# A 16-batch attention and quantised feed-forward kernel: later load slots, a piecewise-contiguous low-rank factor, and a new instruction order

## The chip, the cores and the metric

The kernel runs on one core of one Trainium2 chip. The metric is the device time in microseconds (us) of one execution. Before the change it is 500.97 us, the median of three runs (500.2 to 503.21).

The engines are TensorE (PE, its weight loads are PEld), VectorE (DVE), ScalarE (ACT), GpSimd (POOL) and SyncE (SP), which here only issues DMAs.

## The reference

For 16 batches of x (128 tokens x 512) with a context of 128 x 128:

```python
x = x + attention(layernorm(x), ctx, ctx, q_norm_w, k_norm_w, w_out)   # 16 heads of 32, 4 key heads, rotary, causal
w_up = ((w_up_q - 7.5) * repeat(w_up_scale, 64, axis=1)).T             # 512 x 2048, int32 in memory
y1 = h @ w_up + b_up + h @ w_up_lora_a @ w_up_lora_b                   # h = layernorm(x), rank 16
x2 = relu(y1)
y2 = x2 @ w_down + b_down + x2 @ w_down_lora_a @ w_down_lora_b         # w_down: 2048 x 512, 4 bit likewise
x = x + y2
```

Attention normalises queries and keys by their root mean square, applies the rotary rotation, a causal mask and softmax, and multiplies by w_out.

## The kernel before

**Tiling.** Every float32 product is made of three float16 products (high by high, low by high, high by low). The weights are dequantised once, on the chip, into 32 tiles of 128 x 512: tiles 0 to 15 are the up layer, 16 to 31 the down layer, four tiles to a group of 1 MB that one DMA brings (`load_group`, L346; the staging ring has three places). A weight tile costs: the dequantisation (DVE L1040, or POOL L450 and L453), the turn on PE (`weights`, L801: one low-rank product of 512 columns at L814, then four 128 x 128 float32 transposes at L762 into the same bank), the high part (ACT L615), and the low part, either by DVE (L1048) or by a product with minus the identity (`weights_rest`, L825, product at L830) and a copy on ACT (L620). The low-rank factor of the up layer, `b_up3`, is scaled and split in four pieces by `lora_b_high` (ACT, L604) and `lora_b_low` (DVE, L1023); in its 512 columns the token order is "p then i", and L811 reads it as `(p i) -> i p`, each fourth element.

**Batches.** Each of the 16 batches goes through: statistics, rotary parts, the query and key transposes by DMA (`qT` L396, `kT` L382), four score products S (L856), mask and maximum (DVE L1146), exponentials (ACT L658), probabilities (POOL L480, L489), their transposes by DMA (L406), PV (L872), the output projection PJ (L884, 12 products), the second normalisation and its transpose `xnT` (L389), four up products UP.0 to UP.3 (L902, 12 products of 512 columns each), the hidden layer (DVE L1077, ACT L723, DVE L1086), its transposes (L414), four down products DN.0 to DN.3 (L916, 12 products each), and the store.

**What sets the order.** All engines walk the same counter, `for s in range(SLOTS)`. Each step has a row of slots (`R_...`): three for batches 0 to 2, and one from which batch 3 and all later ones follow every 264 slots. Each weight step has its slot in `TURN_AT`, `DEQ_AT`, `HIGH_AT`, `LOW_AT`, `REST_AT`, `LOAD_AT` and so on. A slot is only a place in the order of an engine's queue; it is no time, and semaphores do the rest. An instruction that waits holds everything behind it on its engine, and on SP a waiting DMA holds the later ones. Below, "W12" is the turn of tile 12 on PE, "S2.1" the second score product of batch 2, and PV1, PJ1, UP1.0, DN0.3 are named the same way.

**The queue of SP.** Before slot 0 SP issues (L356 to L373) batch 0, the small operands, groups 0 and 1, batch 1, group 2, w_out (1 MB), batches 2 and 3, the broadcast bias row (1 MB) and the down bias. Then come the transposes kT0 and qT0; group 3 follows when W3 is done.

**The order of PE** that the tables before give, from PV0 to UP1.0 (sums of squares "v"): PV0, rest 7, rest 8, PJ0, W11, S1.3, W12, v2, W13, W14, W15, rest 12, rest 13, W16, W17, UP0.0, W18, S2.0, W19, S2.1, UP0.1, W20, W21, UP0.2, PV1, W22, S2.2, W23, S2.3, UP0.3, W24, PJ1, W25, DN0.0, W26, W27, DN0.1, W28, W29, S3.0, S3.1, v3, W30, W31, DN0.2, DN0.3, S3.2, UP1.0.

Of the kernel before, what the change touches and what calls it, by code (L numbers as in the profile page):

```python
# [1268 lines left out]
```

## Time and profile before

| | |
|---|---|
| median of three runs | 500.97 us (500.2 to 503.21) |
| the profiled execution, its own time | 503.2 us |
| its span, first to last instruction | 501.4 us |
| PE busy | 458.9 us (92%) |
| DVE, ACT, POOL busy | 343.9 (69%), 303.7 (61%), 292.7 (58%) |
| mean granted TensorE clock | 0.990 |
| PE in the chain that ended last | 85% of the span |

The span is what the rows below are counted in; the execution's own time is 1.8 us more, which lies around it. Row times are from the span's start.

### The profile page before, as it was taken

What the parts mean: (1) busy time and instruction counts of PE and PEld (TensorE: products, weight loads), DVE (VectorE), ACT (ScalarE), POOL (GpSimd) and SP (SyncE); (2) the same over time, 40 slices, a digit from 0 to 9 for tenths busy, and PEclk for the clock granted to TensorE, in tenths of its full rate; (3) what the DMA queues carried; (4) which work ended last, traced back from release to release, by engine and by line L of the source; (5) the groups of instructions that cost most, each with busy time, mean ns of one, the idle gap of its engine ahead of it and who ended that gap; (6) DMA issues with size and microseconds to landing.
All of it is one profiled execution on the core that took longest, in us unless ns stands there. A gap on an engine that the chain in (4) does not pass through costs nothing.

```text
span 501.4 us, 8264 instructions
## 1 busy us (share of the span) xinstructions
PE 458.9 (92%) x2413; PEld 221.6 (44%) x2413; DVE 343.9 (69%) x1082; ACT 303.7 (61%) x927; POOL 292.7 (58%) x304
## 2 busy tenths in 40 slices
PE   0157788999999999999999999999999999999997
PEld 0135434455444444444444444444444444444443
DVE  2759889898768687777777777676767676443341
ACT  1469987568767675757575757676666666521110
POOL 3435764577776758585768585767676756460101
PEclk9999997899999999999999999999999999999999
DMA  7884447936788776777887778778768678474523
GB/s 141 330 242 124 89 151 190 209 74 127 122 173 136 146 138 116 162 127 148 140 148 150 137 150 134 156 125 161 141 143 147 138 118 134 87 136 74 106 46 100
DMA packets 207853, 70.41 MB, mean 140 GB/s; under 512 B 197809, under 2 KB 200113, under 8 KB 207121
## 3 DMA queue, kind: packets, MB, share of 16 engines
q1 hardware_dynamic: 205472, 69.33, 68.4%
q10 hardware_dynamic: 2256, 0.40, 0.5%
q8 instruction: 19, 0.31, 0.3%
q14 instruction: 26, 0.20, 0.1%
q0 software_dynamic: 80, 0.16, 0.1%
HBM read 17.44 MB, written 4.19 MB: 43 GB/s over the span
## 4 chain that ended last, share of the span: by engine, by line
PE 85%; ACT 3%; DVE 2%; DMA 1%; issue 1%; SPq 0%; ACTq 0%
PE ff L916 33%; PE ff L902 33%; PE tb L884 8%; PE ff L762 3%; PE sb L856 3%; PE tb L872 3%; PE ff L814 2%; DMA qT<-q 1%; ACT pr L658 1%; ACT b_row L588 1%; DVE pr L1146 1%; ACT wo_hi L577 0%; PE tb L842 0%; ACT wu_hi L615 0%; DVE wu_lo L1048 0%
## 5 line engine op out<-in xcount | busy, mean ns | idle before, releaser
L902 PE MATMUL ff<-wu_hi,xnT 128*128 128x512 f16 x512 | 153.4, 381 | 0.0
L916 PE MATMUL ff<-wd_hi,x 128*128 128x512 f16 x512 | 152.3, 379 | 0.0
L658 ACT ACTIVATE pr<-pr,nmax 128x128 f32<-128x128 f32 x256 | 99.0, 388 | 33.6 <-DVE nmax L1146 33.3
L1146 DVE CUSTOM_DVE_ANT_0 pr<-sb,tabs,score_scale 128x128 f32<-128x128 f32 x256 | 74.1, 344 | 43.1 <-POOL big L489 22.8
L723 ACT ACTIVATE hid<-z 128x512 f16<-128x512 f32 x64 | 40.2, 628 | 99.0 <-DVE z L1077 99.0
L902 PE MATMUL ff<-wu_lo,xnT 128*128 128x512 f16 x256 | 97.4, 380 | 0.0
L916 PE MATMUL ff<-wd_lo,x 128*128 128x512 f16 x256 | 97.0, 379 | 0.0
L480 POOL TENSOR_TENSOR pr<-pr,rinv 128x512 f32<-128x512 f32 x64 | 72.8, 1152 | 22.1 <-DVE rinv L1056 22.0
L489 POOL TENSOR_TENSOR big<-pr,big 128x512 f16<-128x512 f32 x64 | 75.2, 1185 | 7.7 <-ACT big L689 7.7
L902 PEld LDWEIGHTS ff<-wu_hi,xnT 128*128 128x128 f16 x512 | 48.5, 98 | 59.2 <-issue 7.0
L1077 DVE SCALAR_TENSOR_TENSOR z<-ff,su,b_row 128x512 f32<-128x512 f32 x64 | 47.8, 747 | 37.3 <-PE ff L902 36.0
L916 PEld LDWEIGHTS ff<-wd_hi,x 128*128 128x128 f16 x512 | 49.3, 100 | 51.8
L519 POOL TENSOR_TENSOR inv<-arg,minus_half 128x1 f32<-128x1 f32 x16 | 14.2, 886 | 83.8 <-DVE arg L1132 83.8
L1086 DVE SCALAR_TENSOR_TENSOR hid<-z,hid 128x512 f16<-128x512 f32 x64 | 52.4, 818 | 14.3 <-ACT hid L723 13.2
L658 ACT ACTIVATION_READ_ACCUMULATOR pr<-pr,nmax 128x1 f32 x256 | 48.0, 187 | 0.0
L902 PEld LDWEIGHTS ff<-wu_lo,xnT 128*128 128x128 f16 x256 | 25.1, 98 | 30.6 <-issue 0.6
L916 PEld LDWEIGHTS ff<-wd_lo,x 128*128 128x128 f16 x256 | 25.0, 98 | 30.3
L529 POOL TENSOR_TENSOR y<-x,bd_bc 128x512 f32<-128x512 f32 x16 | 23.7, 1482 | 24.9 <-DMA out<-y 24.8
L689 ACT ACTIVATE big<-pr 128x512 f16<-128x512 f32 x64 | 37.8, 615 | 0.0
L762 PE MATMUL ff<-tabs,big 128*128 128x128 f32 x128 | 29.6, 370 | 2.0 <-DVE big L1040 1.8
L856 PE MATMUL sb<-kT,qT 96*128 96x128 f16 x256 | 24.9, 230 | 5.2 <-DMA qT<-q 5.2
L512 POOL TENSOR_TENSOR t_cos<-xc,cw 128x512 f32<-128x512 f32 x16 | 25.9, 1616 | 3.8 <-ACT xc L629 3.7
(147 smaller groups left out, 622.9 us busy)
## 6 DMA issues: line engine op xcount, KB each, us to landing
xt<-in_x SPq DMA_DIRECT2D x16, 256.0 KB, 3.1
big<-in_L_ffn_w_up_q SPq DMA_DIRECT2D x4, 1024.0 KB, 6.0
big<-in_L_ffn_w_down_q SPq DMA_DIRECT2D x4, 1024.0 KB, 5.6
...
wd_lo<-in_L_xattn_w_out SPq DMA_DIRECT2D x1, 1024.0 KB, 11.7
pT<-in_L_ffn_b_up SPq DMA_DIRECT2D x1, 1024.0 KB, 12.8
pT<-big SPq DMA_TRANSPOSE x64, 3.5
```

The lines of the kernel that those rows point to most:

```text
L480: pool.tensor_tensor(pr[:, m], pr[:, m], rinv[:, p, 4 * m:4 * m + 4].unsqueeze(2).broadcast_to([P, NG, P]), ALU.mult).then_inc(probs, 1)
L489: pool.tensor_tensor(p3[:, m, :, 1, :], pr[:, m], p3[:, m, :, 0, :], ALU.subtract).then_inc(p_low, 1)
L658: last = act.activation(pr[:, m, g, :], pr[:, m, g, :], ACT.Exp, bias=nmax[:, p, j:j + 1], scale=-1.0, accum_out=rsum[:, p, j:j + 1])
L723: act.activation(hid[:, (4 * n + g) % HID_RING, 0, :], z[:, g % 2], ACT.Relu).then_inc(x2_high, 1)
L762: return pe.matmul(dst, src, ident[0:src.shape[0], 0:src.shape[0]], is_transpose=True, **kw)
L856: last = pe.matmul(sbk[m % 2][:, P * g:P * g + P], qT[0:HD3, 4 * m + g, :], kT[0:HD3, g, :], start=True, stop=True)
L884: last = pe.matmul(tb[0][:], a[:, m, :], b[:, m, :], start=(i == 0 and m == 0), stop=(i == 2 and m == NN - 1))
L902: last = pe.matmul(bank[:], a[:, m, :], b[:, m, 512 * g:512 * g + 512], start=(m == 0 and i == 0), stop=(m == KC - 1 and i == 2))
L916: last = pe.matmul(ff[down_bank[n]][:], x2T[:, part, k + h % HG, :], b[:, h, :], start=(h == 0 and i == 0), stop=(h == HC - 1 and i == 2))
L1077: dve.scalar_tensor_tensor(z[:, g % 2], ff[up_bank[n, g]][:], su[:], b_row[:, 512 * g:512 * g + 512], ALU.mult, ALU.add).then_inc(ff_read, 1)
L1086: dve.scalar_tensor_tensor(h[:, 1, :], z[:, g % 2], 0.0, h[:, 0, :], ALU.max, ALU.subtract).then_inc(x2_low, 1)
L1146: last = dve.tensor_tensor_reduce(pr[:, m, g, :], sbk[m % 2][:, P * g:P * g + P], mask, score_scale[:], 3e38, ALU.add, ALU.min, nmax[:, p, ...
```

## The change

Three things change.

1. **Loads.** Group 2, w_out, batches 2 and 3, the bias row and the down bias are no longer issued before slot 0 but in slots of their own. SP's order becomes: batch 0, the small operands, groups 0 and 1, batch 1, then w_out, batch 2, qT0, group 2, kT0, the down bias, the bias row, qT1, kT1, groups 3 and 4, the four pT of batch 0, group 5, kT2, qT2, group 6, xnT0, batch 3, group 7, batch 4.
2. **The low-rank factor.** `b_up3` is written in the order in which it is used, so the product at L814 reads 512 neighbouring elements, and the reordering moves into the source operand of the eight small steps that fill it (L604 and L1023, up pieces).
3. **The order.** All slots are new. DVE dequantises 26 tiles instead of 25 (POOL six instead of seven) and makes 27 low parts instead of 28; the tiles whose low part goes through PE and ACT are 7, 9, 10, 12, 13 instead of 7, 8, 12, 13. No products are added to keep PE busy.

The order of PE from S1.1 to UP1.0 is now: S1.1, S1.2, rest 7, S1.3, W10, rest 9, W11, PV0, W12, W13, rest 10, PJ0, W14, rest 12, W15, v2, W16, W17, S2.0, rest 13, S2.1, W18, W19, S2.2, UP0.0, W20, UP0.1, W21, S2.3, W22, UP0.2, W23, PV1, W24, UP0.3, W25, W26, PJ1, W27, DN0.0, W28, W29, DN0.1, W30, W31, S3.0, v3, S3.1, DN0.2, DN0.3, S3.2, UP1.0.

The diff, cut to its core (the other tables change in the same way):

```diff
-R_SCORES = ((26, 270, 777, 1283), (104, 312, 811, 1320), (119, 390, 924, 1386), (188, 447, 954, 1463))
-R_PV = (412, 879, 1518, 1745)
-R_PROJ = (433, 1065, 1522, 1799)
-R_XNTURN = (705, 1434, 1720, 1991)
-R_UP = ((748, 1406, 1732, 1999), (815, 1471, 1740, 2003), (876, 1504, 1787, 2026), (990, 1519, 1814, 2066))
-R_DOWN = ((1103, 1539, 1886, 2113), (1183, 1546, 1903, 2153), (1363, 1574, 1910, 2191), (1384, 1725, 1922, 2199))
...
+R_SCORES = ((78, 338, 891, 1411), (140, 412, 909, 1440), (198, 451, 980, 1515), (227, 457, 1065, 1544))
+R_PV = (584, 1143, 1556, 1854)
+R_PROJ = (702, 1259, 1615, 1866)
+R_XNTURN = (878, 1405, 1740, 2015)
+R_UP = ((986, 1532, 1788, 2102), (1021, 1535, 1839, 2114), (1097, 1554, 1841, 2119), (1201, 1608, 1865, 2175))
+R_DOWN = ((1286, 1623, 1914, 2216), (1348, 1671, 1962, 2280), (1458, 1694, 2012, 2289), (1500, 1710, 2039, 2306))
...
-DVE_TILES = (0, 1, 2, 3, 4, 5, 6, 7, 8, 9, 11, 15, 16, 17, 18, 19, 20, 21, 22, 23, 24, 25, 27, 28, 29)
-LOW_BY_DVE = (0, 1, 2, 3, 4, 5, 6, 9, 10, 11, 14, 15, 16, 17, 18, 19, 20, 21, 22, 23, 24, 25, 26, 27, 28, 29, 30, 31)
-TURN_AT = (14, 37, 40, 111, 215, 310, 325, 339, 366, 407, 411, 443, 457, 551, 562, 602, 707, 719, 773, 780, 830, 863, 906, 935,
-           991, 1097, 1142, 1160, 1236, 1277, 1344, 1357)
-HIGH_AT = (58, 73, 271, 276, 306, 367, 422, 451, 499, 546, 618, 684, 726, 782, 797, 810, 834, 840, 890, 942, 965, 966, 1037,
-           1088, 1147, 1158, 1193, 1224, 1285, 1292, 1316, 1329)
-REST_AT = (0, 0, 0, 0, 0, 0, 0, 427, 432, 0, 0, 0, 679, 702, 0, 0, 0, 0, 0, 0, 0, 0, 0, 0, 0, 0, 0, 0, 0, 0, 0, 0)
-LOAD_AT = (20, 484, 595, 711, 855)
-LORA_TURN_AT = (2, 4, 15)
-LORA_BHIGH_AT = (8, 9, 10, 364, 517)
-LORA_BLOW_AT = (8, 15, 25, 472, 603)
-WO_TURN_AT = (162, 170, 236, 256)
-WO_HIGH_AT = (129, 146, 193, 256)
-BIAS_ROW_AT = (171, 253, 296, 316)
-WO_SQUARES_AT, WO_SUM_AT, WO_ARG_AT, WO_POW_AT = 11, 6, 17, 7
...
+DVE_TILES = (0, 1, 2, 3, 4, 5, 6, 7, 8, 10, 11, 12, 13, 14, 15, 17, 18, 19, 21, 23, 25, 26, 27, 28, 29, 31)
+LOW_BY_DVE = (0, 1, 2, 3, 4, 5, 6, 8, 11, 14, 15, 16, 17, 18, 19, 20, 21, 22, 23, 24, 25, 26, 27, 28, 29, 30, 31)
+TURN_AT = (67, 115, 121, 215, 253, 350, 352, 356, 388, 410, 463, 550, 586, 612, 778, 803, 873, 877, 910, 953, 992, 1058, 1070,
+           1115, 1150, 1207, 1242, 1277, 1313, 1318, 1383, 1409)
+HIGH_AT = (76, 187, 192, 203, 217, 356, 369, 380, 410, 442, 516, 587, 626, 697, 751, 772, 843, 859, 943, 1014, 1058, 1113, 1169,
+           1201, 1262, 1359, 1395, 1445, 1469, 1478, 1501, 1581)
+REST_AT = (0, 0, 0, 0, 0, 0, 0, 453, 0, 530, 663, 0, 796, 900, 0, 0, 0, 0, 0, 0, 0, 0, 0, 0, 0, 0, 0, 0, 0, 0, 0, 0)
+LOAD_AT = (61, 462, 490, 770, 861, 906)
+WO_LOAD_AT, ROW_LOAD_AT, DOWN_BIAS_LOAD_AT = 2, 262, 169
+BATCH_LOAD_AT = (3, 881)
+LORA_TURN_AT = (2, 6, 108)
+LORA_BHIGH_AT = (8, 9, 40, 41, 453)
+LORA_BLOW_AT = (15, 24, 73, 117, 513)
+WO_TURN_AT = (174, 175, 207, 289)
+WO_HIGH_AT = (104, 107, 188, 226)
+BIAS_ROW_AT = (167, 266, 290, 357)
+WO_SQUARES_AT, WO_SUM_AT, WO_ARG_AT, WO_POW_AT = 13, 3, 34, 132
...
@@ -291,7 +293,8 @@
             if by_dve:
                 eng.wait_ge(w_low_v, by_dve)
 
-        b_pieces = [(b_up3[:, 512 * i:512 * i + 512], b_up_in[:, 512 * i:512 * i + 512], 4) for i in range(4)] + [(b_dn3, b_dn_in, 5)]
+        b_pieces = [(b_up3[:, 512 * i:512 * i + 512].rearrange("k (i p) -> k i p", i=4),
+                     b_up_in[:, 512 * i:512 * i + 512].rearrange("k (p i) -> k i p", i=4), 4) for i in range(4)] + [(b_dn3, b_dn_in, 5)]
 
 
         tile_bank, up_bank, down_bank, tile_free, up_free, down_free = {}, {}, {}, {}, {}, {}
@@ -365,12 +368,6 @@
             load_group(0)
             load_group(1)
             load_batch(1)
-            load_group(2)
-            sp.dma_start(wo_raw, wo.rearrange("(j p) c -> p j c", p=P)).then_inc(wout_in, 16)
-            load_batch(2)
-            load_batch(3)
-            sp.dma_start(bias_raw, bu.rearrange("(a n) -> a n", a=1).broadcast_to([P, H])).then_inc(bias_row_in, 16)
-            sp.dma_start(bd_bc[:], bd.rearrange("(a n) -> a n", a=1).broadcast_to([P, C])).then_inc(down_bias_in, 16)
             sp.wait_ge(parts_empty, 2)
             for s in range(SLOTS):
                 n = at(s, R_KTURN)
@@ -412,9 +409,18 @@
                         if n > 0:
                             sp.wait_ge(down_done, n)
                         sp.dma_start_transpose(x2T[:, g], hid[:, (4 * n + g) % HID_RING].rearrange("p a h -> p (a h)")).then_inc(x2_turned[g], 16)
-                for g in range(W_RING, 8):
-                    if LOAD_AT[g - W_RING] == s:
+                for g in range(2, 8):
+                    if LOAD_AT[g - 2] == s:
                         load_group(g)
+                if s == WO_LOAD_AT:
+                    sp.dma_start(wo_raw, wo.rearrange("(j p) c -> p j c", p=P)).then_inc(wout_in, 16)
+                for n in (2, 3):
+                    if BATCH_LOAD_AT[n - 2] == s:
+                        load_batch(n)
+                if s == ROW_LOAD_AT:
+                    sp.dma_start(bias_raw, bu.rearrange("(a n) -> a n", a=1).broadcast_to([P, H])).then_inc(bias_row_in, 16)
+                if s == DOWN_BIAS_LOAD_AT:
+                    sp.dma_start(bd_bc[:], bd.rearrange("(a n) -> a n", a=1).broadcast_to([P, C])).then_inc(down_bias_in, 16)
                 n = at(s, R_STORE)
                 if n is not None:
                     store(n)
@@ -808,7 +814,7 @@
                     pe.wait_ge(b_high, t // 4 + 1)
                     pe.wait_ge(b_low, t // 4 + 1)
                 if t < UP_TILES:
-                    a, b = a_up3[:, P * j:P * j + P], b_up3[:, 512 * g:512 * g + 512].rearrange("k (p i) -> k i p", i=4)
+                    a, b = a_up3[:, P * j:P * j + P], b_up3[:, 512 * g:512 * g + 512]
                 else:
                     a, b = (a_dn3[:], a_dn3_late)[t // 24][:, P * (t % 8):P * (t % 8) + P], b_dn3
                 pe.matmul(bank[:], a, b, start=True, stop=False, skip_group_check=True)
```

## Rows read from the trace of the kernel before

**Rows 1.** Busy time by stretch: length, PE, PEld, DVE, ACT, POOL, clock, DMA

```profile
36.00:60.00 24.00, 17.54 (x75) 12.02 (x74) 21.42 (x73) 22.78 (x66) 14.23 (x15) 1.00 0.36 90
60.27:82.25 21.98, 20.57 (x88) 10.17 (x89) 18.32 (x38) 17.72 (x45) 12.14 (x14) 0.84 0.56 154
82.25:125.64 43.39, 41.64 (x223) 21.94 (x221) 38.12 (x115) 30.70 (x95) 28.75 (x32) 0.96 0.75 150
125.64:498.15 372.51, 372.28 (x1999) 172.87 (x1996) 246.59 (x790) 217.77 (x696) 222.03 (x216) 1.00 0.71 132
```

**Rows 2.** The chain that ended last, in order of time

```profile
79.46 7.38 DMA qT<-q
...
101.44 2.59 PE ff L902 x12
...
105.03 2.59 PE tb L884 x12
...
190.40 0.45 PE sb L856 x8
...
498.15 0.75 DVE y L1196
```

**Rows 3.** What PE waited for in the first 130 us

```profile
PE sb L856 <- DMA qT<-q: 5.2, 3, 2.3
PE sb L774 <- ACT big L571: 3.7, 1, 3.7
```

**Rows 4.** PE in order of time: start, length, step

```profile
63.33 0.61 PE L814 MATMUL ff<-wd_lo,wd_hi 48*128 48x512 f16 x1
63.87 1.12 PE L762 MATMUL ff<-tabs,big 128*128 128x128 f32 x4
...
66.31 1.03 PE L830 MATMUL ff<-wu_hi,minus 128*128 128x512 f16 x2
67.81 1.04 PE L884 MATMUL tb<-wo_hi,oT_hi 128*128 128x512 f16 x4 [0.46 <-DVE oT_lo L1167]
...
72.88 0.61 PE L814 MATMUL ff<-wd_lo,wd_hi 48*128 48x512 f16 x1 [0.95 <-ACT wu_lo L620]
73.41 0.66 PE L762 MATMUL ff<-tabs,big 128*128 128x128 f32 x4
...
87.35 0.38 PE L856 MATMUL sb<-kT,qT 96*128 96x128 f16 x4 [1.35 <-DMA qT<-q]
...
93.11 0.39 PE L814 MATMUL ff<-wd_hi,a_dn 48*128 48x512 f16 x1
...
94.11 0.39 PE L814 MATMUL ff<-wd_hi,a_dn 48*128 48x512 f16 x1
```

**Rows 5.** PE by stretch: length, busy, granted clock, DMA

```profile
75.00:76.00 1.00, 1.00 (x5) 0.50 0.93 363
```

**Rows 6.** The low-rank product of line L814, by form: ns min/median/max

```profile
L814 PE MATMUL ff<-wd_lo,wd_hi x16: 606/607/609, 30.4 to 77.3; 48*128 48x512 f16 x16
L814 PE MATMUL ff<-wd_hi,a_dn x8: 386/387/605, 79.7 to 100.2; 48*128 48x512 f16 x8
```

**Rows 7.** ACT from 20 to 100 us, by line and form

```profile
L588 ACT ACTIVATE b_row<-pT,kap 128x512 f32<-128x512 f32 x4 | 4.8, 1201 | 0.0
L604 ACT ACTIVATE wd_lo<-wd_hi,kap 48x512 f16<-48x512 f32 x4 | 2.6, 706 | 0.0
```

**Rows 8.** SP's queue in order of time

```profile
24.36 8.15 SPq L396 DMA_TRANSPOSE qT<-q  x1
...
78.98 0.37 SPq L350 DMA_DIRECT2D big<-in_L_ffn_w_down_q  x1
```

**Rows 9.** DMA issues by line: KB each, median us to landing

```profile
qT<-q SPq DMA_TRANSPOSE x16, 4.4
xnT<-xn_parts SPq DMA_TRANSPOSE x16, 3.1
wd_lo<-in_L_xattn_w_out SPq DMA_DIRECT2D x1, 1024.0 KB, 11.7
```

More of the change, by code:

```diff
@@ L68 @@
[L68 to L73 removed]
+R_STATS = (0, 6, 40, 928)
+R_SQUARES = (2, 6, 280, 1133)
@@ new lines @@
+R_MOMENTS = (0, 12, 220, 1073)
+R_KEYS = (0, 4, 202, 1453)
+R_POW = (2, 19, 463, 1494)
+R_CENTRE = (3, 44, 376, 1227)
+R_SINES = (2, 44, 308, 1194)
+R_COSINES = (3, 57, 625, 1592)
+R_ROPE = (3, 46, 437, 1215)
+R_KSPLIT = (4, 154, 441, 1334)
+R_KLOW = (4, 85, 421, 1235)
+R_KTURN = (85, 439, 799, 1300)
+R_QSPLIT = (5, 117, 574, 1376)
+R_QLOW = (5, 77, 557, 1262)
+R_QTURN = (54, 380, 806, 1253)
+R_SCORES = ((78, 338, 891, 1411), (140, 412, 909, 1440), (198, 451, 980, 1515), (227, 457, 1065, 1544))
@@ new lines @@
+R_MASK = ((35, 258, 702, 1446), (50, 319, 716, 1459), (121, 386, 996, 1471), (159, 560, 1122, 1537))
+R_EXP = ((98, 444, 1057, 1586), (169, 500, 1112, 1599), (262, 742, 1329, 1663), (340, 862, 1373, 1772))
+R_SUMS = ((49, 415, 1146, 1490), (86, 556, 1175, 1530), (173, 570, 1366, 1661), (233, 788, 1448, 1713))
+R_PROBS = ((182, 651, 1595, 1911), (193, 657, 1599, 1925), (411, 879, 1645, 2013), (484, 1099, 1839, 2080))
+R_PHIGH = ((207, 673, 1374, 1691), (229, 815, 1449, 1753), (375, 995, 1557, 1842), (390, 1080, 1592, 1861))
@@ new lines @@
+R_PLOW = ((327, 737, 1621, 1947), (379, 973, 1628, 1964), (564, 1300, 1790, 2038), (577, 1382, 1857, 2136))
+R_PTURN = ((509, 1062, 1273, 1748), (634, 1135, 1412, 1769), (694, 1143, 1435, 1774), (706, 1148, 1471, 1780))
+R_VSUM = (337, 398, 849, 1432)
+R_VARG = (172, 283, 945, 1507)
+R_VPOW = (456, 649, 1837, 2135)
+R_VSPLIT = (393, 1189, 1603, 1871)
+R_VLOW = (623, 1432, 1859, 2177)
+R_PV = (584, 1143, 1556, 1854)
+R_OHIGH = (530, 1209, 1708, 1941)
+R_OLOW = (515, 1147, 1567, 1829)
+R_PROJ = (702, 1259, 1615, 1866)
@@ new lines @@
+R_X1 = (567, 1323, 1652, 1909)
+R_POW2 = (794, 1632, 2010, 2252)
+R_YBASE = (1840, 2031, 2200, 2702)
+R_XN = (777, 1480, 1805, 2085)
+R_XNLOW = (590, 1435, 1678, 1980)
+R_XNTURN = (878, 1405, 1740, 2015)
+R_UP = ((986, 1532, 1788, 2102), (1021, 1535, 1839, 2114), (1097, 1554, 1841, 2119), (1201, 1608, 1865, 2175))
+R_Z = ((984, 1476, 1766, 2049), (992, 1527, 1792, 2080), (1120, 1541, 1810, 2157), (1304, 1648, 1879, 2227))
+R_X2HIGH = ((1188, 1602, 1921, 2190), (1264, 1698, 1956, 2268), (1346, 1731, 1997, 2285), (1476, 1774, 2063, 2309))
@@ L101 @@
+WO_HIGH_AT = (104, 107, 188, 226)
+WO_LOW_AT = (52, 65, 127, 143)
+LORA_A_AT, LORA_ALOW_AT = 7, 9
+BIAS_ROW_AT = (167, 266, 290, 357)
+WO_SQUARES_AT, WO_SUM_AT, WO_ARG_AT, WO_POW_AT = 13, 3, 34, 132
 RING, W_RING, HID_RING = 4, 3, 3
```

60 lines of the change are left out of this document (11 added, 49 removed).

## The prediction, made before the changed kernel ran

> **What bounds the kernel now.** I read the stretches first, then the chain, then what PE waits for, then single rows. From 125.64 us, where UP1.0 starts, to 498.15 PE is busy 372.28 of 372.51 us at the full clock [rows 1], and the chain ends with the last down products and one 0.75 us step of DVE [rows 2]. The list of PE products in that stretch is the same in both tables (what stands ahead of UP1.0 before stands ahead of it now), and DVE at 246.59 and POOL at 222.03 us have room in it. So the change is worth what it moves UP1.0, no more, unless the new periodic order makes a wait that recurs.
>
> Ahead of UP1.0 there are two stages. From 36 to 60 us ACT is busy 22.78 of 24 us, DVE 21.42, PE only 17.54 [rows 1]: ACT and DVE bind, and PE waits for them and for the first transposes: 5.2 us in three waits for qT and 3.7 for the squares of w_out are the largest [rows 3]. From 60.27 on PE is busy 20.57 of 21.98 us and then 41.64 of 43.39 [rows 1]: it binds, but at mean granted clocks of 0.84 and 0.96.
>
> The clock needs care. The column says 1.0 until its first change, but the rows before it contradict that: the four transposes of W10 (63.87) took 1.12 us, those of W12 (73.41) took 0.66, so the first ran at the lower level of 1.2 GHz, the second at 2.4 [rows 4]. The rise lies where dense work stood: at 66.31 two products of 512 columns took 1.03 us, at 67.81 four of the same width took 1.04 [rows 4]. At 75 us the column gives 0.50 with PE busy all of that microsecond [rows 5]; just before, PE had waited 0.95 us and then turned tiles [rows 4]. Seen from product to product, a turned down tile costs 1.00 us at the full level (94.11 - 93.11) [rows 4], and at the half level an up tile costs 0.54 + 1.04, 1.58 us (63.33 to 63.87, then the 1.12 of the transposes less some 0.08 of overlap with the next) [rows 4].
>
> **The change, part by part.**
>
> *The order from UP0.0 to UP1.0.* Prices at full clock: UP, DN and PJ 2.59 each, a score product 0.45 / 2 = 0.22 [rows 2], a tile 1.00 [rows 4]; PV 0.8 and v3 0.3 are small and equal on both sides. Before: 8 x 2.59 + 2.59 + 14 x 1.00 + 7 x 0.22 + 1.1 = 39.95 us of work in the 43.39 us of that stretch [rows 1], so 3.4 us are lost, of which 1.35 is the wait of S2.0 for qT2 [rows 4] and the rest is half clock around 88 to 91 us and small waits. Now W18, W19, S2.0, S2.1 and S2.2 stand ahead of UP0.0: 2 x 1.00 + 3 x 0.22 = 2.7 us less work behind it. The 1.35 us wait goes too, since qT2 is no longer issued behind group 6 (it took 7.38 us there [rows 2], 4.4 in the median [rows 9]). Together 4.05 us. The other 2.1 us of loss I keep.
>
> *What lies ahead of UP0.0.* I keep UP0.0 at 82.3 us, as before (82.25), from terms of both signs.
> - Earlier: the loads. qT0 was issued at 24.36, held SP for 8.15 us [rows 8], and its scores started about 2 us behind its issue's end, at 34.7. Five transfers, some 2.6 MB, were ahead of it that are now behind it. Its landing then costs between the 4.4 us of the median and the 8.15 and more of now; but kT0 now stands behind group 2, and a transpose right behind a 1 MB load took 7.38 us [rows 2] against 4.4 in the median [rows 9]. I take S0.0 at 32.5, 2.2 us earlier (bounds 0 and 5). W_out, which took 11.7 us to land [rows 9], no longer follows group 2, and its squares (the 3.7 us wait [rows 3]) come up to 2.5 us earlier; three reorderings of 0.5 us now stand before them on ACT, which takes back 1.5.
> - Later: on ACT, the first two high parts of w_out stand ahead of the second and third exponentials. They wait for the turns of w_out, which on PE stand behind five other steps, each at half clock (a tile 1.58): about 2 us of ACT, the binding engine of this stage, go here. PV0 and PJ0 then come at about 64 and 68.5 us (before 64.9 and 67.8), with W11 to W13 and S1.3, 3.2 us of PE work at full clock, already done.
> - From PJ0's end PE has W14 to W19, three scores, two rests: 6 x 1.00 + 1.4 = 7.4 us at full clock, 6 x 1.58 + 2.0 = 11.5 at half. 71.5 plus that is 78.9 to 83.0; xnT0 lands at about 81 (the second norm 8.5 us behind PJ0 as before, then 3.1 [rows 9]), or later behind group 6, which SP now issues just ahead of it (before, group 6 went at 78.98, after it [rows 8]): bounds 3.1 and 7.4 us. I take 82.3, nearest to the usual landing; the bounds are 80 and 86.
>
> *The low-rank factor in one piece.* L814 takes 606 ns in all 16 up tiles, also in the three that ran at the full level (72.88 is one), and 386 in the down tiles, whose factor is contiguous; at the half level a contiguous one takes 605 too [rows 6]. So the strided read costs 0.22 us a tile, at full clock alone: between 0 (all half) and 16 x 0.22 = 3.5 us. At most four or five up tiles will run at full clock, 1 us, and they lie in the stage where PE still waits for banks. I take 0. The reordering moves to the source of four small steps on ACT and four on DVE: the strided scaling of the bias row takes 1201 ns against 706 for the plain one [rows 7], so 0.5 us a piece, 2.0 us on ACT (bounds 0 and 2.0); for DVE no row shows it, I bound it by the same 0 and 2.0. Two pieces of each fall before 29 us, when both engines wait anyway; the others are inside the 2 us of delay taken above. Where that cover is gone they cost 1 us on each.
> The Trainium skill (SBUF — State Buffer, Door 1: The DMA port swizzle) says that SBUF is read in lines of 16 bytes and that two hits in a line suffice, so that each fourth float16 should be read at full rate. The trace does not agree: 606 against 386 ns [rows 6]. By that rule the contiguous factor would save nothing at any clock; by the row up to 3.5 us; the sum above holds 0 either way.
>
> *Low parts and tiles.* One low part leaves DVE (0.6 us) for a product on PE (0.22) and a copy on ACT, one dequantisation comes to DVE (0.6): nothing within 0.3 us. The remaining SP edits (batch 3, biases) have more than 10 us of room.
>
> **Sum.** The profiled execution took 503.2 us (span 501.4 and 1.8 around it). UP1.0 moves from 125.64 to 121.6: 503.2 - 4.05 = 499.2. That execution lies 2.2 above the median of the runs; against the median the forecast is 500.97 - 4.05 = 496.9, taken as **497.0 us**.
>
> **The rivals.**
> 1. *Full clock from PJ0 on.* If no wait on PE between 68 and 90 us lets the clock fall, the tiles end by 79 us, UP0.0 starts with xnT0 at 80, and the 2.1 us of kept loss go too: 4.05 + 2.3 + 2.0 = 8.3 us, 492.7. For it: contiguous tiles put less time into sparse work. Against: the tile stage of before fell to 0.50 after a wait of 0.95 us [rows 4, 5], and ACT and DVE, not PE, set its pace.
> 2. *Half clock through PJ0, the tiles and UP0.1 (slower).* Before, the clock rose only at PV0 and two dense rest products, the two of 66.31 [rows 4]. Now these are spread among tiles and waits for high parts. If the rise misses them, PJ0 costs 2.6 us more, W14 to W21 8 x 0.58 = 4.6, UP0.0 and UP0.1 5.2: 12.4 us. 2.3 of it hides in waits, 4.05 is gained: 6 us slower, 507. It decides from 4 us lost on. For it: PE stayed at half for the whole stretch from 30 to 66 us though from 36 on it was busy 17.54 of 24 us [rows 1]. Against: PV0, W12, W13 and PJ0 stand as close together as their counterparts did.
> 3. *xnT0 behind group 6, or DVE the bound.* xnT0 at 7.4 us lands near 85.5; UP0.0 loses 3 us of the 4: 500.0. DVE reaches the same place: it must do about 36 of the next 39.3 us, 91% against 88% (38.12 of 43.39 [rows 1]).
>
> **Chances.** Forecast 0.40, rival 1 0.25, rival 2 0.17, rival 3 0.18. A measurement can tell about 1%, 5 us, from no change. Faster by over 1% (below 496): nearly all of rival 1 and a third of the forecast's own spread, 0.38. Slower by over 1%: most of rival 2 and a recurring wait in the period, 0.16. Within: 0.46. The range runs from rival 1's outer end, 490.5, to 505.5, which leaves out half of rival 2.
>
> **What would show it.** UP1.0's first product near 121.6 us and PE busy without gaps behind it; UP0.0 near 82; S0.0 near 32.5; L814 at about 386 ns where the granted clock is full and 606 where not; L604's first four steps near 1200 ns; S2.0 without a wait for qT2. I am wrong if UP0.0 comes before 80 or after 86, if PJ0 takes 5.2 us, if the stretch behind UP1.0 is not 372.5 us, or if qT0 lands as late as before.

## The result, and the profile after

The changed kernel takes 497.1 us, the median of five runs (497.02 to 497.91). The kernel before takes 501.19 us in five runs beside them (500.2 to 503.21). The ratio is 0.9899, with a 95% interval of 0.9869 to 0.9929: some 4 us, 1%, faster. The forecast was 497.0. As the next parts show, the forecast came this close because two of its terms were wrong by about the same amount, with opposite signs.

One thing first, since every comparison of start times below needs it. The kernel before was run and profiled once more, unchanged.

```diff
(no edit: the kernel before)
```

> The kernel before once more, for a second profiled execution. If the order explains the gain (theory O) and the first profiled execution only started late, the first group's load is issued nearer 11.4 than 13.0 us here, UP1.0 starts at about 124 instead of 125.64 us, and the stretch from UP0.0 to UP1.0 is again 43.4 us within 0.5. If that stretch varies from run to run by more than 1 us, the comparison of the two traces proves less than it seems to.

Measured: a median of 501.24 us in ten runs (500.28 to 504.83), ratio 1.0001 (0.9977 to 1.0026). The new profiled execution took 500.9 us and its span 499.1. Its stages have the lengths of the first one, but everything stands about 2.2 us earlier: UP0.0 at 80.00 (first profile 82.25), UP1.0 at 123.59 (125.64), the last step at 495.85 (498.15). The queue of SP shows where the 2.2 us lie, in the first issue of a weight group, which follows the small operands. The row from the first profile of before:

```profile
12.99 0.82 SPq L350 DMA_DIRECT2D big<-in_L_ffn_w_up_q  x2
```

the same from the second profile of before:

```profile
10.79 0.82 SPq L350 DMA_DIRECT2D big<-in_L_ffn_w_up_q  x2
```

and from the changed kernel:

```profile
11.35 0.82 SPq L353 DMA_DIRECT2D big<-in_L_ffn_w_up_q  x2
```

The start up to that issue varies by 2.2 us between executions of one program. So the execution behind the prediction was long by its start, as the prediction's sum had assumed in bulk, and the second profile is the one to set beside the changed kernel: both lie within 0.4 us of their own medians.

The changed kernel by stretches (columns as in [rows 1]). The steps of PE, DVE and ACT now stand six lines further down (L814 is L820, L902 is L908), SP's transposes three lines up (qT is L393), and the experiments' kernels have line numbers of their own.

```profile
60.00:81.76 21.76, 20.68 (x96) 11.12 (x97) 18.43 (x58) 18.73 (x58) 13.20 (x14) 0.69 0.82 189
81.76:119.44 37.68, 37.22 (x201) 19.07 (x199) 36.11 (x90) 27.66 (x83) 26.37 (x29) 1.00 0.70 143
119.44:491.98 372.54, 372.30 (x1999) 172.84 (x1996) 244.38 (x788) 219.19 (x697) 211.14 (x217) 1.00 0.72 132
```

The stretch from UP0.0 to UP1.0 in the second profile of before:

```profile
80.00:123.59 43.59, 41.63 (x222) 21.97 (x220) 38.10 (x115) 30.68 (x95) 28.73 (x32) 0.96 0.74 149
```

Read them together. The last stretch is 372.54 us with PE busy 372.30, where it was 372.51 and 372.28 [rows 1]: nothing changed behind UP1.0. The stretch ahead of it shrank from 43.59 to 37.68 us, 5.91. UP0.0 came later, at 81.76 instead of 80.00, 1.76. The difference is 4.15, and the two executions' own times differ by 500.9 - 497.02 = 3.88.

PE of the changed kernel in order of time: two early tiles, PV0, PJ0, the tiles behind it, UP0.0, UP0.1 and PV1:

```profile
32.60 0.39 PE L820 MATMUL ff<-wd_lo,wd_hi 48*128 48x512 f16 x1
...
41.72 0.60 PE L820 MATMUL ff<-wd_lo,wd_hi 48*128 48x512 f16 x1
...
64.57 1.47 PE L878 MATMUL tb<-pT,v 128*32 128x512 f16 x12 [0.37 <-issue]
...
69.43 1.39 PE L890 MATMUL tb<-wo_hi,oT_hi 128*128 128x512 f16 x4
...
75.19 0.39 PE L820 MATMUL ff<-wd_hi,a_dn 48*128 48x512 f16 x1 [0.49 <-DVE wu_lo L1054]
75.79 0.75 PE L768 MATMUL ff<-tabs,big 128*128 128x128 f32 x4 [0.21 <-DVE big L1046]
...
78.08 0.63 PE L836 MATMUL ff<-wu_hi,minus 128*128 128x512 f16 x1
...
81.76 0.61 PE L908 MATMUL ff<-wu_hi,xnT 128*128 128x512 f16 x2
...
85.36 0.59 PE L908 MATMUL ff<-wu_hi,xnT 128*128 128x512 f16 x2
...
93.85 0.83 PE L878 MATMUL tb<-pT,v 128*32 128x512 f16 x12
```

PJ0 begins at the lower level (four products in 1.39 us) and turns to the full one. A single rest product takes 0.63 us at 78.08, so the clock has fallen again, behind two short waits. Two products of UP0.0 take 0.61 us at 81.76 and two of UP0.1 0.59 at 85.36: full clock. A window tells the same of 78 to 80 us (columns: length, busy time of PE, PEld, DVE, ACT, POOL, then clock, DMA share, GB/s):

```profile
78.00:80.00 2.00, 2.00 (x11) 1.09 (x10) 1.77 (x9) 2.00 (x9) 1.83 (x3) 0.50 1.58 265
```

In the kernel before, the stretch from UP0.0 on went otherwise. Rows of its first profile behind the wait of S2.0 [rows 4]:

```profile
87.98 1.04 PE L762 MATMUL ff<-tabs,big 128*128 128x128 f32 x4
88.81 0.63 PE L856 MATMUL sb<-kT,qT 96*128 96x128 f16 x4
89.24 1.06 PE L902 MATMUL ff<-wu_hi,xnT 128*128 128x512 f16 x2
90.09 0.63 PE L902 MATMUL ff<-wu_lo,xnT 128*128 128x512 f16 x1
```

There the wait of 1.35 us is followed by some 3.7 us at the lower level. Step by step the lower level costs 1.04 - 0.75 for the transposes, 0.63 - 0.39 for the score, and 3.87 - 2.69 for UP0.1 (89.24 to 93.11 here, 85.36 to 88.05 in the changed kernel): 1.7 us.

What PE waits for in the first 130 us of the changed kernel (columns as in [rows 3]; the two largest, 14.0 and 8.9 us, stand ahead of 25 us, much as before):

```profile
PE tb L848 <- DVE wo_lo L1040: 4.1, 1, 4.1
PE tb L768 <- DVE wo_lo L1040: 3.2, 1, 3.2
PE sb L780 <- ACT big L577: 3.0, 1, 3.0
```

The three waits for qT, 5.2 us in all [rows 3], are gone. In their place PE waits for parts of w_out that DVE makes, all ahead of 50 us, where PE doesn't bind. SP's queue shows the reason that the qT waits are gone, in the rows of qT0, group 2 and kT0 and in those of qT2, group 6 and xnT0 (between them stand the four transposes of batch 0's probabilities, pT0):

```profile
22.03 1.43 SPq L393 DMA_TRANSPOSE qT<-q  x1
23.51 1.28 SPq L353 DMA_DIRECT2D big<-in_L_ffn_w_up_q  x1
24.89 1.19 SPq L379 DMA_TRANSPOSE kT<-k  x1
...
54.62 7.80 SPq L403 DMA_TRANSPOSE pT<-big  x4
...
68.54 1.32 SPq L393 DMA_TRANSPOSE qT<-q  x1
...
74.61 0.37 SPq L353 DMA_DIRECT2D big<-in_L_ffn_w_down_q  x1
...
77.44 1.23 SPq L386 DMA_TRANSPOSE xnT<-xn_parts  x1
...
81.66 0.38 SPq L353 DMA_DIRECT2D big<-in_L_ffn_w_down_q  x1
...
83.26 7.64 SPq L403 DMA_TRANSPOSE pT<-big  x4
```

qT0 holds SP for 1.43 us instead of 8.15 [rows 8]. Five of the transfers that stood ahead of it now stand behind. By the profile's time from issue to landing, it took 4.9 us instead of 10.3, and qT2 4.5 instead of 7.4.

The new queue costs something too. Group 4 now goes right ahead of the four pT0 (54.13), which hold SP for 7.80 us. In both profiles of before no load stood there, and they took 5.36. The last is issued by 62.42, and PV0 starts 2.15 us later, at 64.57, behind a wait of 0.37 us. Four variants of the changed kernel below, of which the profiles show a wait at the same place (0.22 to 1.29 us), have 2.12 to 2.15 us there too. So SP sets the date of PV0 in all five. In the kernel before PE didn't wait there. xnT0 likewise took 4.3 us from issue to landing, against 3.0 in both profiles of before: it lands at about 81.7, when PE is just done with the steps ahead of UP0.0 (81.76).

Last, the low-rank factor. Its product in the lines by form from 20 to 100 us (busy us, mean ns, idle before):

```profile
L820 PE MATMUL ff<-wd_lo,wd_hi 48*128 48x512 f16 x16 | 8.8, 550 | 0.0
```

The same product, and the four small steps on ACT and the four on DVE that now do the reordering (ns min/median/max):

```profile
L820 PE MATMUL ff<-wd_lo,wd_hi x16: 386/604/607, 29.6 to 73.6; 48*128 48x512 f16 x16
...
L610 ACT ACTIVATE wd_lo<-wd_hi,kap x4: 1196/1202/1236, 22.3 to 29.5; 48x512 f16<-48x512 f32 x4
...
L1029 DVE SCALAR_TENSOR_TENSOR wd_lo<-wd_hi,kap,wd_lo x4: 1112/1128/1922, 25.6 to 43.2; 16x512 f16<-16x512 f32 x4
```

The product now takes 386 ns where the clock is full and about 604 where it is half. Its mean over the 16 up tiles is 550 ns, against 606 before [rows 6], so PE saves 16 x 0.056 = 0.9 us in all. ACT pays 0.50 us a step (1202 against 706 [rows 7]). DVE, for which no row of before gave a price, pays 0.39 (1128 against 741, the median of the same four steps in the kernel before; in the run below that puts the old form back it is 760).

### The profile page after: what moved, and what is told of

Its sections match the earlier page's. It is cut to its first block, busy times and chain, and to the rows that moved or that the text cites. A ratio compares the mean times of both kernels' runs of the same rounds, so it can differ in the third digit from the quotient of the medians.

```text
span 495.2 us, 8264 instructions
## 1 busy us (share of the span) xinstructions
PE 455.0 (92%) x2414; PEld 219.6 (44%) x2414; DVE 345.7 (70%) x1082; ACT 307.0 (62%) x928; POOL 281.2 (57%) x302
## 4 chain that ended last, share of the span: by engine, by line
PE 83%; DVE 7%; DMA 1%; SPq 1%; issue 1%; ACT 0%
PE ff L908 33%; PE ff L922 31%; PE tb L890 8%; PE ff L768 3%; PE sb L862 3%; PE tb L878 3%; PE ff L820 2%; DVE big L1046 1%; DMA x<-hid 1%; DVE pr L1152 1%; DVE t_sin L1120 1%; DVE wd_lo L1029 1%; DVE hid L1092 1%; DVE wu_lo L1054 1%; DVE wd_lo L1054 0%
## 5 line engine op out<-in xcount | busy, mean ns | idle before, releaser
L908 PE MATMUL ff<-wu_hi,xnT 128*128 128x512 f16 x512 | 152.5, 379 | 0.0
L495 POOL TENSOR_TENSOR big<-pr,big 128x512 f16<-128x512 f32 x64 | 80.6, 1267 | 47.3 <-ACT big L695 47.0
L908 PE MATMUL ff<-wu_lo,xnT 128*128 128x512 f16 x256 | 97.0, 379 | 0.0
L908 PEld LDWEIGHTS ff<-wu_hi,xnT 128*128 128x128 f16 x512 | 48.3, 98 | 58.7 <-issue 5.9
L1092 DVE SCALAR_TENSOR_TENSOR hid<-z,hid 128x512 f16<-128x512 f32 x64 | 54.8, 857 | 11.8 <-ACT hid L729 11.8
L695 ACT ACTIVATE big<-pr 128x512 f16<-128x512 f32 x64 | 39.9, 623 | 16.1 <-POOL pr L486 16.1
L645 ACT ACTIVATE q<-q,inv 128x1024 f16<-128x1024 f32 x16 | 18.3, 1146 | 35.9 <-DVE q L1069 35.6
L908 PEld LDWEIGHTS ff<-wu_lo,xnT 128*128 128x128 f16 x256 | 25.0, 98 | 30.3
L535 POOL TENSOR_TENSOR y<-x,bd_bc 128x512 f32<-128x512 f32 x16 | 20.7, 1293 | 22.5 <-DMA out<-y 22.5
L768 PE MATMUL ff<-tabs,big 128*128 128x128 f32 x128 | 28.6, 360 | 0.2 <-DVE big L1046 0.2
```

The lines of the kernel that those rows point to most:

```text
L495: pool.tensor_tensor(p3[:, m, :, 1, :], pr[:, m], p3[:, m, :, 0, :], ALU.subtract).then_inc(p_low, 1)
L695: act.activation(p3[:, m, :, 0, :], pr[:, m], ACT.Copy).then_inc(p_high, 1)
L768: return pe.matmul(dst, src, ident[0:src.shape[0], 0:src.shape[0]], is_transpose=True, **kw)
L908: last = pe.matmul(bank[:], a[:, m, :], b[:, m, 512 * g:512 * g + 512], start=(m == 0 and i == 0), stop=(m == KC - 1 and i == 2))
L1092: dve.scalar_tensor_tensor(h[:, 1, :], z[:, g % 2], 0.0, h[:, 0, :], ALU.max, ALU.subtract).then_inc(x2_low, 1)
```

## The experiments

Times are medians. "Before" in the ratios is the kernel before, run on the same chip beside each experiment: 501.49 us (33 runs), 501.81 (23) and 501.71 (28) in the three sets. As the single executions of one kernel spread by 1 to 6 us, single profiles are used for where something stands, and ratios for what it is worth.

**The factor as before, in the changed kernel.**

```diff
-        b_pieces = [(b_up3[:, 512 * i:512 * i + 512].rearrange("k (i p) -> k i p", i=4),
...
+        b_pieces = [(b_up3[:, 512 * i:512 * i + 512], b_up_in[:, 512 * i:512 * i + 512], 4) for i in range(4)] + ...
-                    ..., b_up3[:, 512 * g:512 * g + 512]
+                    ..., b_up3[:, 512 * g:512 * g + 512].rearrange("k (p i) -> k i p", i=4)
```

> The changed kernel with the low-rank factor laid out as before (strided read on PE, plain source on ACT and DVE). Theory O, and the prediction, which took 0 for this part: 497 us within 0.7. Theory C (the contiguous factor carries the gain, 0.22 us for each up tile that runs at full clock): the changed kernel shows the full level in two up tiles ahead of 39 us and in two behind PJ0, so 0.4 to 0.9 us, and more if the shorter products keep the clock up: 498 to 501 us.

Measured: 497.93 us in ten runs (495.56 to 501.54), ratio 0.9917 (0.9886 to 0.9948). UP0.0 stands at 82.88, UP1.0 at 120.60. The product takes 607 ns in all 16 tiles again, at either level, as [rows 6] said. The time is that of the changed kernel within what ten such runs can tell.

**The contiguous factor alone, in the kernel before.** The same edit the other way round.

```diff
+        b_pieces = [(b_up3[:, 512 * i:512 * i + 512].rearrange("k (i p) -> k i p", i=4),
...
+                    ..., b_up3[:, 512 * g:512 * g + 512]
```

> The kernel before with the contiguous low-rank factor alone. Theory O: three up tiles run at full clock there, 0.6 us at most, partly under waits, and ACT has 2 us more to do in its fullest stage: 500.5 to 502.5, no difference. Theory C: a gain of 1 to 4 us, 497 to 500.

Measured: 502.24 us in twelve runs (500.98 to 504.37), ratio 1.0003 (0.9981 to 1.0025). So this part of the change is worth nothing that the runs can tell, in either order, as the prediction took it. An effect below about 1 us stays open.

**The loads at the front again, in the changed kernel.**

```diff
             load_batch(1)
+            load_group(2)
+            sp.dma_start(wo_raw, ...)
+            load_batch(2)
+            load_batch(3)
+            sp.dma_start(bias_raw, ...)
+            sp.dma_start(bd_bc[:], ...)
             sp.wait_ge(parts_empty, 2)
```

> The changed kernel with group 2, w_out, batches 2 and 3 and both biases issued ahead of slot 0, as before. Theory L (the load slots carry the gain): the first scores come back to about 34 us, and all behind them, some 2 to 4 us are lost, 499 to 501. Theory O: the first scores come later by the same 2 to 3 us, but low parts of w_out and ACT set PV0 and PJ0, so at most 1 us is lost: 497 to 498.

Measured: 499.42 us in twelve runs (498.88 to 500.24), ratio 0.9953 (0.9934 to 0.9972). This gives back about 2 us of the 4. On SP, qT0 holds the queue as long as it did before (8.15 [rows 8]):

```profile
23.06 6.83 SPq L399 DMA_TRANSPOSE qT<-q  x1
```

S0.0 comes at 32.59 instead of 31.06, PJ0 at 70.97 instead of 69.43, UP0.0 at 84.06 instead of 81.76. The stretch from UP0.0 to UP1.0 is 37.85 us, as short as in the changed kernel. So the loads act on what lies ahead of UP0.0.

The same run shows the order without the loads, since its first weight load (10.90) is as early as in the second profile of before (10.79). The order shortens the stretch from UP0.0 to UP1.0 by 5.74 us (43.59 to 37.85) and brings UP0.0 4.06 us later (80.00 to 84.06), 1.68 us in all.

**The load slots alone, in the kernel before.** W_out and batch 2 stay ahead of slot 0; group 2 goes between qT0 and kT0, and the biases and batch 3 behind them.

```diff
-            load_group(2)
             sp.dma_start(wo_raw, ...)
             load_batch(2)
...
+                if s == 2:
+                    load_group(2)
+                if s == 4:
+                    (down bias, bias row, batch 3)
-R_QTURN = (3, 56, 747, 1263)
+R_QTURN = (1, 56, 747, 1263)
-R_KTURN = (2, 125, 751, 1266)
+R_KTURN = (3, 125, 751, 1266)
```

> The kernel before with the load slots alone: w_out, batch 2, qT0, group 2, kT0, both biases, batch 3, all else in the old order. Moved back to the front in the changed kernel, the loads cost 2.3 us (499.42 against 497.1). If the load slots are a gain in themselves (theory L), 498.5 to 499.5 us. If they pay only in the new order, which has ACT and DVE work ready for scores that come early (theory O), 500.5 to 501.5, no difference.

Measured: 500.09 us in six runs (499.11 to 500.72), ratio 0.9962 (0.9948 to 0.9976), 1.9 us faster. S0.0 stands at 30.65 and UP0.0 at 78.75, 1.25 earlier than in the second profile of before, 1.9 if both are counted from the first weight load (11.43 and 10.79). Part of that is lost again behind it, at half clock in UP0.0 and behind a wait of 1.62 us at PV1: UP1.0 stands at 123.16, 0.43 earlier (1.07 counted from the load). The 1.9 us rest on the ratio, not on this profile. Both ways round the loads are worth some 2 us, and the new order some 2 us without them.

**UP0.0 later, in the kernel before.** W18, S2.0, W19 and S2.1 go ahead of it: four of the five steps that the prediction priced at 2.7 us.

```diff
-R_UP = ((748, 1406, 1732, 1999), ...
+R_UP = ((812, 1406, 1732, 1999), ...
```

> The kernel before with UP0.0 moved behind W18, S2.0, W19 and S2.1 on PE, nothing else. If the 5.8 us that the stretch from UP0.0 to UP1.0 lost come from PE's order there (theory O in its narrow form, the 2.7 plus 1.35 us of the prediction): the wait for qT2 is then met before UP0.0 in work that it can't cover, UP0.0 starts 4 to 6 us later and UP1.0 at the same time: 501 to 503. So the gain would need ACT, DVE and SP to be ahead too, not the order of PE alone. If the order of PE alone is enough: 497.5 to 499.5.

Measured: 505.96 us in six runs (504.17 to 506.54), ratio 1.0075 (1.0058 to 1.0092): slower. PE in order of time:

```profile
83.37 0.60 PE L814 MATMUL ff<-wd_hi,a_dn 48*128 48x512 f16 x1 [1.96 <-DVE wd_lo L1048]
...
86.95 0.58 PE L856 MATMUL sb<-kT,qT 96*128 96x128 f16 x4 [1.92 <-DMA qT<-q]
...
89.35 1.06 PE L902 MATMUL ff<-wu_hi,xnT 128*128 128x512 f16 x2
```

The steps that were pulled ahead wait for DVE and for qT2, 3.9 us in all, and UP0.0 then starts at the lower level (two products in 1.06 us), 9.35 us later than in the second profile of before (8.1 counted from the first weight load). The stretch behind it does shrink by what the prediction's prices give, 3.83 us (43.59 to 39.76, with UP1.0 at 129.11) against 2.44 for the four steps and 1.35 for the wait; what stands ahead of it takes more than that. "The work is done earlier, so there is less behind" holds only where its inputs are ready.

**UP0.0 earlier, in the changed kernel.** It goes ahead of S2.0, rest 13, S2.1, W18, W19 and S2.2.

```diff
-R_UP = ((986, 1532, 1788, 2102), ...
+R_UP = ((890, 1532, 1788, 2102), ...
```

> The changed kernel with UP0.0 moved ahead of S2.0, rest 13, S2.1, W18, W19 and S2.2. By the prediction PE then waits for xnT0 from about 77.7 to 80.7 us and the 2.7 us of products come behind it: 1.5 to 3 us slower than the changed kernel, 498.5 to 500. If xnT0 lands early enough to start UP0.0 in that gap, no difference: 497 within 0.7.

Measured: 503.63 us in twelve runs (501.18 to 505.21), ratio 1.0019 (0.9999 to 1.0039): 6.5 us over the changed kernel by the medians, 5.6 to 6.0 by the ratios.

```profile
81.49 1.04 PE L908 MATMUL ff<-wu_hi,xnT 128*128 128x512 f16 x2 [3.06 <-DMA xnT<-xn_parts]
...
86.16 0.39 PE L862 MATMUL sb<-kT,qT 96*128 96x128 f16 x4
...
89.51 0.39 PE L820 MATMUL ff<-wd_hi,a_dn 48*128 48x512 f16 x1 [0.29 <-DVE wd_lo L1054]
90.71 0.75 PE L768 MATMUL ff<-tabs,big 128*128 128x128 f32 x4 [0.81 <-DVE big L1046]
```

xnT0 lands hardly earlier, so UP0.0 starts at 81.49 all the same, now behind a wait of 3.06 us. It then runs at half clock until it ends at 86.16, 4.67 us instead of 2.70, and the steps that had filled the wait still have to be done. UP1.0 moves by 125.85 - 119.44 = 6.4 us, the whole loss. Most of it is there at UP0.1, which starts at 91.29 instead of 85.36, 5.9 later: 2.9 us of steps that had filled the gap (86.16 to about 89.1), 2.0 of clock in UP0.0, and 1.1 of waits for DVE.

**qT2 ahead of group 6, in the kernel before.** This removes the 1.35 us wait by itself.

```diff
-LOAD_AT = (20, 484, 595, 711, 855)
+LOAD_AT = (20, 484, 595, 752, 855)
```

> The kernel before with group 6's load behind qT2 and kT2 on SP, nothing else. The transpose then issues at about 78.2 us and lands 4.4 us later, so S2.0's wait of 1.35 us goes, and perhaps the fall of the clock behind it (another 1.5 us): 498.5 to 500.2 us if the prediction's term is right. If UP0.0's end (84.9 us) and the tile behind it hide qT2 anyway, or the load comes too late for group 6's tiles, 501 within 1.

Measured: 503.3 us in twelve runs (501.35 to 505.33), ratio 1.0026 (1.0003 to 1.0049): no gain. The wait is gone (S2.0 at 83.87 without one), and so is the half clock behind it: UP0.1 runs from 85.31 to 88.00, 2.69 us. But PV1 comes later than it did in the row of 98.16 below, and it waits. This run:

```profile
96.32 1.41 PE L872 MATMUL tb<-pT,v 128*32 128x512 f16 x12 [3.67 <-issue]
```

The first profile of before:

```profile
98.16 0.83 PE L872 MATMUL tb<-pT,v 128*32 128x512 f16 x12 [0.40 <-issue]
```

The label "issue" names no releaser. SP's queue of this run gives it: the transposes of batch 1's probabilities, pT1, stand right behind groups 6 and 7.

```profile
81.39 0.57 SPq L350 DMA_DIRECT2D big<-in_L_ffn_w_down_q  x1
82.07 5.31 SPq L406 DMA_TRANSPOSE pT<-big  x2
87.43 1.14 SPq L350 DMA_DIRECT2D big<-in_L_ffn_w_down_q  x1
88.67 5.23 SPq L406 DMA_TRANSPOSE pT<-big  x2
```

They hold SP for 5.31 and 5.23 us, so the last is issued by 93.9, and PV1 follows 2.4 us later. In the first profile of before the last one was issued by 95.8, and PV1 followed 2.4 us later too:

```profile
90.62 5.17 SPq L406 DMA_TRANSPOSE pT<-big  x2
```

So PV1 had stood close to a date that SP sets. In all six profiles of the old order in which PV1 waits, this one included, it starts 2.36 to 2.47 us behind the last issue of pT1. The load that no longer stands ahead of qT2 stands ahead of pT1. PE reached it at 92.65 instead of 97.76, some 3 us sooner when the start's 1.96 us are taken off, and waited there. Behind the wait of 3.67 us the clock was at the lower level again: PV1's twelve products took 1.41 us, not 0.83.

**Load slots and qT2 together, in the kernel before.**

```diff
(the edit of the load slots, and)
-LOAD_AT = (20, 484, 595, 711, 855)
+LOAD_AT = (20, 484, 595, 752, 855)
```

> The load slots (1.9 us on their own) and qT2 ahead of group 6, both in the old order. If the two terms add and carry the change, 497 to 498.5, the changed kernel's time without its new order. If the rest of the order is needed for the stretch from UP0.0 to UP1.0 to shrink (43.4 to 37.7 us), it stays at 499 to 500.

Measured: 501.91 us in twelve runs (498.47 to 503.16), ratio 0.9995 (0.9974 to 1.0016). The 1.9 us of the load slots are gone too: PV1 waits for 3.52 us. With the load slots alone it waited 1.62. The changed kernel doesn't wait there, for two reasons that its rows above show: qT2 is issued at 68.54 and both loads by 81.66, ahead of all four pT1 (83.26); so that the last is issued by 90.90 (92.02 in this run, 93.90 in the one above); and three tiles and a score stand beside UP0.2 between UP0.1 and PV1, where the old order has two tiles, so that PV1 comes at 93.85. How much each of the two gives was not tested by itself.

**The low part of the factor later, in the changed kernel.** This tests whether the 0.39 us a step on DVE (theory D) delays the stage.

```diff
-LORA_BLOW_AT = (15, 24, 73, 117, 513)
+LORA_BLOW_AT = (15, 24, 182, 352, 513)
```

> The changed kernel with two of the four strided low parts of the low-rank factor (DVE, 1.13 and 1.92 us at 40.3 and 43.2 us) moved later in DVE's order, behind the low part of tile 3 and the dequantisation of tile 15. If DVE's queue there carries the wait of 4.1 us that PE has for the last low part of w_out (theory D: the contiguous factor's price on DVE lies on the path), PV0 and UP0.0 come 1 to 3 us earlier: 494 to 496. If the half clock and ACT set the pace behind it, 497 within 0.7.

Measured: 499.86 us in twelve runs (496.96 to 501.52), ratio 0.9948 (0.9927 to 0.9968): 2 to 3 us slower than the changed kernel. In its profile new waits stand at PJ0 and UP0.0:

```profile
PE tb L890 <- DVE oT_lo L1173: 1.8, 1, 1.8
PE ff L908 <- DMA xnT<-xn_parts: 1.5, 1, 1.5
```

That theory falls: nothing came earlier. But the two waits don't explain the loss. PJ0 starts at 69.60 (69.43 in the changed kernel), xnT0 is issued at 77.25 (77.44), and UP0.0 starts at 81.91, only 0.15 us later. UP1.0 is 1.78 us later (121.22), and 1.64 of that lies in UP0.0 itself, which runs mostly at half clock behind its wait (4.34 us to W20, not 2.70).

**PJ0 earlier, in the changed kernel.**

```diff
-R_PROJ = (702, 1259, 1615, 1866)
+R_PROJ = (600, 1259, 1615, 1866)
```

> The changed kernel with PJ0 moved ahead of W13 and rest 10 on PE: its input is ready at 67.7 us and PE gets to it at 69.4. If the dense products of PV0 and PJ0 standing closer together raise the clock 1.5 to 2 us sooner, the tiles behind them run at full clock and UP0.0 starts 1 to 2 us earlier: 495 to 496.5. If PE's list ahead of UP0.0 is the bound and the clock does not rise sooner: 497 within 0.7.

Measured: 500.48 us in twelve runs (497.59 to 503.66), ratio 0.9963 (0.9938 to 0.9989): about 3 us slower than the changed kernel. PJ0 starts 1.66 us earlier, but wholly at half clock:

```profile
67.77 1.89 PE L890 MATMUL tb<-wo_hi,oT_hi 128*128 128x512 f16 x4 [0.16 <-DVE oT_lo L1173]
69.45 1.91 PE L890 MATMUL tb<-wo_hi,oT_lo 128*128 128x512 f16 x4
```

It takes 4.6 us (67.77 to 72.35) instead of 3.05 (69.43 to 72.48). It ends at the same time, so starting it earlier brought nothing, and W13 and rest 10, which had been done ahead of it, now come behind. The chain that ended last shows what that delays:

```profile
73.36 0.60 ACT wu_hi L621
...
74.44 1.53 ACT pr L664 x8
```

ACT had waited 4.15 us for the transposes of W13 before that high part. What stands behind it in ACT's order, exponentials and high parts, comes later, and with it the second norm (L714, at 77.54 instead of 75.11). xnT0 is issued at 79.89 instead of 77.44, lands at about 84.1, and UP0.0 stands at 84.14 (81.76). UP1.0 is 2.48 us later (121.92), nearly all of the loss in this profile. So the run's price is that of W13 coming late for ACT. It doesn't show what an earlier rise of the clock would give.

**The changed kernel once more.**

```diff
(no edit: the changed kernel)
```

> The changed kernel once more, as the yardstick for its own variants: 497.1 within 0.5 us, with the strided factor's 497.9 and the later low parts' 499.9 to be read against it. If its runs scatter over 5 us as theirs do, neither difference counts.

Measured: 497.32 us in six runs (496.4 to 498.91), ratio 0.9908 (0.9881 to 0.9935). Its profiled execution issued the first weight group 1.4 us later than the first one (12.72 against 11.35), and yet UP0.0 stands at 81.52 and UP1.0 at 119.19. Its clock was full from about 67 us on, and PE waited for xnT0:

```profile
81.52 0.60 PE L908 MATMUL ff<-wu_hi,xnT 128*128 128x512 f16 x2 [1.35 <-DMA xnT<-xn_parts]
```

What PE gained by the clock, the landing of xnT0 took (4.5 us from its issue at 76.97). In the first profile PE and xnT0 are ready within about 0.1 us of each other, in the second xnT0 is later. So xnT0 bounds UP0.0 in both: a better clock behind PJ0 would have gained next to nothing. It is also what PE waits for ahead of UP0.0 with the strided factor (1.41 us), the loads at the front (1.12), and the later low parts (1.45).

None of the variants beats the changed kernel. Its form with the strided factor isn't told apart from it.

## Why the prediction was right, and where only its sum was

- **What decides.** That the steady stretch stays at 372.5 us and only the place of UP1.0 counts held: 372.54 us, and 4.15 us of movement of UP1.0 against 3.88 of time.
- **The stretch from UP0.0 to UP1.0: too small a gain.** The prediction took off 4.05 us and kept 2.1 us of other loss. The work of its sum, 39.95 - 2.7 = 37.25 us, fills the measured 37.68 us to 0.43. So the kept loss nearly went, by 1.7 us. The step that failed is "the rest is half clock around 88 to 91 us": this was put down as independent, though the rows have it right behind the wait for qT2. The run with qT2 ahead of group 6 shows them going together, since its UP0.1 took 2.69 us. The rest of the kept loss is the wait of 0.40 us at PV1. That the clock fell behind the wait is what happened here, not a rule: behind 1.35 us at UP0.0 in the second profile of the changed kernel it stayed full.
- **The same stretch: terms that don't stand alone.** The 2.7 us and the 1.35 us were summed as if each edit earned its own. Alone they gain nothing: the ratio is 1.0075 with UP0.0 late, 1.0026 with qT2 first. The prediction didn't ask what is late next once the wait for qT2 is gone; it was PV1, behind the pT1 transposes. In the changed kernel both terms pay. Its traces show SP's queue ahead in time and more PE work ahead of PV1, and which of the new slots are needed for that wasn't tested.
- **UP0.0: later, not unchanged.** The forecast was 82.3 against 82.25, no movement. Against the second profile of before it moved by +1.76 us, of which 0.56 is the later first load. The earlier half of the term held: S0.0 comes 1.4 us earlier (32.45 to 31.06), 1.95 with the first load as zero, where 2.2 was taken. The later half was too small, and PV0 is the step that was put wrong: 0.9 us earlier (64 against 64.9), when it came 1.90 later (62.67 to 64.57). PE itself reaches it at 64.20, behind steps at half clock and a wait of 1.23 us for DVE at 60.00. The pT0 transposes behind group 4, which the prediction doesn't mention, add 0.37, and up to 1.29 in the variants. From PV0 to PJ0 it took 1.6 us more and 1.95 came, tiles and a rest at half clock. So PJ0 came 3.85 later (65.58 to 69.43), where 0.7 was taken. From PJ0 to UP0.0 2.1 us came back (14.42 to 12.33), where 0.6 was taken. How much earlier PV0 would come with pT0 free of the load wasn't tested.
- **The sum.** The stretch gave -5.91 us where -4.05 was forecast, UP0.0 +1.76 where 0 was: errors of -1.86 and +1.76, which cancel. That 497.0 lies so close is chance; that it lies in the range isn't, since both errors are inside the bounds given.
- **The loads.** They were priced as "S0.0 2.2 us earlier" and then given away to ACT. The runs give them about 2 us of the kernel's time, both when taken from the changed kernel and when put into the old one.
- **The low-rank factor.** Its value of 0 held within about 1 us. 0.9 us of PE time is saved, where the prediction put at most 1 us. The prices were 0.50 us a step on ACT, as read from L588 [rows 7], and 0.39 on DVE, 1.6 us for its four steps, inside the bounds. The Trainium skill (SBUF — State Buffer, Door 1: The DMA port swizzle) would have the strided read free; both orders with the strided form have it at 606 or 607 ns, so the measurement decides against that reading for a moving operand of PE.
- **Rival 1** (full clock from PJ0 on, 492.7) came true in one part: the loss behind UP0.0 went. The clock fell to 0.50 once more at 77 to 80 us in the first profile, and in the second, where it didn't, xnT0 was late. Its time needed UP0.0 at 80, with xnT0, and xnT0 landed no earlier than 81.4 in any profile of the new order.
- **Rival 2** (half clock through PJ0 and on, 507) came true in another: PJ0 starts at half clock. In the run with PJ0 earlier it runs at half clock nearly throughout, 4.6 us, but the tiles right behind it and UP0.0 are at full clock. No run shows the rival's 12.4 us.
- **Rival 3** (xnT0 behind group 6) came in small. Group 6 was issued at 74.61, xnT0 at 77.44, and it took 4.3 us to land, not the 7.4 of the rival and not the 3.0 of before. That is 1.3 us on the chain that UP0.0 hangs on. Whether group 6 is the cause stays open: in the run with UP0.0 earlier group 6 stood as close ahead of it (75.50 and 78.33), and it took 3.1. That DVE would bind fell too: it is busy 36.11 us, as predicted, but of 37.68, and PE waits for it once there, 0.46 us.

What stays open is what sets the moment at which the clock rises. In the first profile of the changed kernel it was full from 32.6 to about 39.3 us, then half until PJ0 (its rows at 32.60, 41.72 and 69.43), and half again from 77 to 80; in the second it was full from 67 on, with the same two short waits of 0.5 and 0.2 us ahead of 76. Nor is it shown when a wait lets it fall. It stayed full behind 1.35, 1.41 and 1.12 us at UP0.0 (second profile, strided factor, loads at the front). It was half behind 1.45 us at the same place (later low parts), and fell within some 1.1 us behind 1.35 us at S2.0 and 1.62 at PV1 (kernel before, load slots alone). The runs of orders that differ by one step (PJ0, the low parts) spread over 6.1 and 4.6 us, those of the changed kernel over 0.9 and 2.5.
